# Decoder on one Trainium2 core: the masked-expert stage in two halves of the rows

## The reference

```python
# graph (_L0_xattn_ref): result is added to x, then layer norm
threshold = top_k(sim, 76)[0][:, :, -1:]
A_learned = sigmoid(sim) * (sim >= threshold)
A_learned = (A_learned + swapaxes(A_learned, -1, -2)) * 0.5
return (1.0 - gamma) * adj_raw + gamma * A_learned          # adj_raw is x
# experts (_L0_ffn_ref)
logits = einsum('bsd,ed->bse', x, router_w)
top1_w, top1_idx = max(softmax(logits)), argmax(softmax(logits))
w_q = clip(round(weight / 0.5), -1, 1) * scale[:, None]
out[token] = top1_w * (x[token] @ (w_q * expert_masks[top1_idx]).T)
```

## Time and profile before

| | |
|---|---|
| time, median of 3 runs | 870.21 us (869.89 to 872.01) |
| the profiled execution | 870.9 us |
| its span, first to last instruction | 869.1 us |
| TensorE busy | 790.7 us, 91% |
| VectorE busy | 572.8 us, 66% |
| ScalarE busy | 422.1 us, 49% |
| GpSimd busy | 498.7 us, 57% |
| mean granted TensorE clock | 0.968 |
| chain that ended last | PE 66%, DVE 14%, issue 7%, POOL 5% |

### The profile page before, as it was taken

The page is one execution under the profiler, slowest core; times in us unless marked ns, Lnnn a source line. Parts: engine busy times, 40 slices in busy tenths (PEclk is TensorE's granted clock), DMA queues, the critical chain, the costliest instruction groups (busy, mean ns, idle before and its releaser), DMA issues.

```text
span 869.1 us, 14599 instructions
## 1 busy us (share of the span) xinstructions
PE 790.7 (91%) x4731; PEld 678.7 (78%) x4737; DVE 572.8 (66%) x1661; ACT 422.1 (49%) x1193; POOL 498.7 (57%) x407
## 2 busy tenths in 40 slices
PE   8999999999999876794899989999985899999995
PEld 5878898888888864492788878898874588888884
DVE  5796876967768486123778878786737645455555
ACT  3473644636446564171475745766754532323232
POOL 6667468647587351512585546356512387776763
PEclk9999999999999997797999999999999899999998
DMA  7121620222316112555020111010001011111111
GB/s 215 66 98 35 208 97 1 97 68 80 123 35 194 62 56 68 193 113 140 0 79 3 54 55 56 1 55 26 25 1 38 13 55 36 54 36 54 46 32 49
DMA packets 58332, 59.09 MB, mean 68 GB/s; under 512 B 5392, under 2 KB 49312, under 8 KB 58272
## 3 DMA queue, kind: packets, MB, share of 16 engines
q1 hardware_dynamic: 57504, 56.24, 20.8%
q0 software_dynamic: 768, 2.10, 0.8%
HBM read 50.00 MB, written 8.32 MB: 67 GB/s over the span
## 4 chain that ended last, share of the span: by engine, by line
PE 66%; DVE 14%; issue 7%; POOL 5%; DVEq 2%; ACT 2%; DMA 2%; POOLq 1%; SPq 0%
PE bank L126 15%; PE bank L128 15%; PE bank L127 15%; PE bank L913 4%; PE bank L946 4%; PE bank L907 3%; PE bank L927 3%; DVE bank L1174 2%; PE bank L947 2%; POOL a_queries L755 2%; DVEq L1221 2%; DVE a_top L1223 1%; PE bank L1652 1%; PE bank L1653 1%; DVE sim L1149 1%
## 5 line engine op out<-in xcount | busy, mean ns | idle before, releaser
L1054 ACT ACTIVATE a_probs<-bank,a_neg_peak 128x128 f32<-128x128 f32 (+1 forms) x256 | 103.5, 429 | 96.2 <-DVE a_neg_peak L1174 96.2
L1174 DVE CUSTOM_DVE_ANT_0 bank<-bank,causal 128x128 f32<-128x128 f32 (+1 forms) x256 | 82.6, 390 | 34.2 <-PE bank L907 32.8
L1082 ACT ACTIVATE a_probs<-a_probs,a_row_inv 128x128 f32<-128x128 f32 (+1 forms) x256 | 92.1, 454 | 11.2 <-DVE a_row_inv L1182 11.2
L1060 ACT ACTIVATE a_probs_t<-bank 128x512 f32<-128x512 f32 x96 | 54.1, 601 | 60.3 <-PE bank L927 60.3
L946 PE MATMUL bank<-a_probs_t,a_vals 128*128 128x256 f32 x256 | 77.7, 386 | 3.3 <-DVE a_ot_lo L1194 3.3
L1909 POOL TENSOR_TENSOR d_h_lo<-d_h,d_h_hi 128x512 fp32r<-128x512 f32 x40 | 51.7, 1294 | 45.5 <-ACT d_h_hi L2029 31.9
L755 POOL TENSOR_TENSOR a_queries<-sim 128x512 f32<-128x512 f32 x32 | 41.0, 1283 | 62.3 <-DVE sim L1149 62.3
L126 PE MATMUL bank<-a_wo_hi,a_ot_hi 128*128 128x256 f32 x256 | 72.8, 284 | 4.3 <-issue 4.3
L2115 DVE TENSOR_TENSOR d_h<-d_silu,bank 128x512 f32<-128x512 f32 x40 | 27.5, 688 | 71.9 <-PE bank L128 70.5
L128 PE MATMUL bank<-a_wo_hi,a_ot_lo 128*128 128x256 f32 x256 | 71.7, 280 | 0.0
L127 PE MATMUL bank<-a_wo_lo,a_ot_hi 128*128 128x256 f32 x256 | 71.6, 280 | 0.0
(11 more groups left out here) (328 smaller groups left out, 2410.1 us busy)
## 6 DMA issues: line engine op xcount, KB each, us to landing
d_raw<-in_L_ffn_we_dram SPq DMA_DIRECT2D x48, 128.0 KB, 2.2
raw_k<-in_L_attn_w_k_dram SPq DMA_DIRECT2D x8, 512.0 KB, 7.4
raw_q<-in_L_attn_w_q_dram SPq DMA_DIRECT2D x8, 512.0 KB, 6.4
raw_v<-in_L_attn_w_v_dram SPq DMA_DIRECT2D x8, 512.0 KB, 7.6
raw_o<-in_L_attn_w_o_dram SPq DMA_DIRECT2D x8, 512.0 KB, 3.6
kv<-_L_ffn_expert_masks_dram SPq DMA_DIRECT2D x16, 256.0 KB, 3.0
kvt<-_L_ffn_expert_masks_dram SPq DMA_DIRECT2D x16, 256.0 KB, 3.1
raw_o<-in_L_attn_Wo_dram SPq DMA_DIRECT2D x8, 512.0 KB, 3.6
```

The lines of the kernel that those rows point to most:

```text
L1054: nc.scalar.activation(probs[s % 2][:, i, at:at + width], c.banks[i][:, at:at + width], ACT.Exp, bias=neg_peak[:, n:n + 1], scale=-1.0, ac ...
L1082: last = nc.scalar.activation(part, part, ACT.Copy, scale=row_inv[:, s % 2, n + r:n + r + 1])
L1174: last = nc.vector.tensor_tensor_reduce(part, part, mask, -1.0, 3e38, ALU.add, ALU.min, neg_peak[:, n + r:n + r + 1])
```

## The change

The rows are grouped in halves. Each half has its own sorted list (`sorted_rows[h]`, `y_sorted[h]`), of 39 tiles and five chunks, so there are ten chunks and 78 tiles. A class `Grouping` holds the steps of the chain for one half.

Half 0's chain moves into the first attention, to the ends of steps: constants and the first tanh (6), keep (7), turns, symmetric and the moments (8), first_norm (9), second_norm (10), turn of x (11), raw router products and flatten (12), logits and choose (13), rank, put, weigh and find (14); GpSimd scatters it in step 15, ahead of its last masks. The units use the ring. In the masked stage half 1's chain runs beside the weight turns and the first chunks; its scatter lies beside half 0's chunks; half 0's gather, sums and norm lie beside half 1's chunks. The keep_warm calls of the stage are gone, the products' banks are three instead of four, bank 3 serves the router.

```diff
+KEPT_STEP, FLAT_STEP, X_STEP, LOGITS_STEP, RANK_STEP = 8, 12, 11, 13, 14
+EARLY = {KEPT_STEP: ("kept", 0, range(B // 2)), X_STEP: ("turn", 0, range(KC)), FLAT_STEP: ("raw", 0, range(1)),
+         LOGITS_STEP: ("logits", 0, range(1)), RANK_STEP: ("rank", 0, range(1))}
...
@@ attention, SyncE @@
-                if not rope and g == 2:
-                    blank = c.idle[:].bitcast(F32).unsqueeze(1).broadcast_to([P, CHUNKS * BANK // P, D])
-                    sp.dma_start(c.sorted_rows.rearrange("(t p) d -> p t d", p=P), blank).then_inc(c.s_blank, 16)
+                if not rope and g == 1:
+                    sp.dma_start(grouping.numbers[:], a["numbers"][:, 0:HALF_NT]).then_inc(grouping.s_numbers, 16)
+                if not rope and g in (2, 3):
+                    blank = c.idle[:].bitcast(F32).unsqueeze(1).broadcast_to([P, HALF_CHUNKS * BANK // P, D])
+                    sp.dma_start(c.sorted_rows[g - 2].rearrange("(t p) d -> p t d", p=P), blank).then_inc(c.s_blank[g - 2], 16)
...
@@ attention, GpSimd, in step s, ahead of masks(s) @@
                 if not rope and s == 9:
                     ternary()
+                    pool.drain()
+                    grouping.norm1.root(pool, 0, factor=c.less_sq[:])
+                if not rope and s == 10:
+                    grouping.norm2.root(pool, 0)
+                if not rope and s == LAST:
+                    grouping.scatter(pool, 0)
...
@@ attention, TensorE, at the end of step s @@
+                if s == KEPT_STEP:
+                    kept_transposes(0)
+                elif s == X_STEP:
+                    for k in range(KC):
+                        grouping.turn(pe, 0, k, claim("turn", 0, k), s_early_t)
+                elif s == FLAT_STEP:
+                    pe.wait_ge(s_taken, taken("turn", 0, KC - 1))
+                    grouping.raw(pe, 0, claim("raw", 0, 0))
+                elif s == LOGITS_STEP:
+                    grouping.logits(pe, 0, claim("logits", 0, 0))
+                elif s == RANK_STEP:
+                    grouping.rank(pe, 0, claim("rank", 0, 0))
...
@@ attention, ScalarE, at the end of step s @@
+                if s == KEPT_STEP - 2:
+                    tanh(0)
+                elif s == X_STEP:
+                    for k in range(KC):
+                        act.wait_ge(s_early_t, k + 1)
+                        nc.scalar.activation(c.xt_hi[:, k, 0:HALF], ring_bank("turn", 0, k)[:], ACT.Copy).then_inc(s_early_hi, 1)
+                elif s == FLAT_STEP:
+                    grouping.flatten(act, 0, ring_bank("raw", 0, 0))
+                elif s == LOGITS_STEP:
+                    tanh(1)
+                elif s == RANK_STEP:
+                    grouping.exp(act, 0)
...
@@ attention, VectorE, at the end of step s @@
+                if s == KEPT_STEP - 2:
+                    grouping.constants(dve)
+                elif s == KEPT_STEP - 1:
+                    keep(0)
+                elif s == KEPT_STEP:
+                    symmetric(0)
+                    grouping.norm1.moments(dve, lambda t: c.x[:, t], 0)
+                elif s == KEPT_STEP + 1:
+                    grouping.first_norm(dve, 0)
+                elif s == KEPT_STEP + 2:
+                    grouping.second_norm(dve, 0)
+                elif s == X_STEP:
+                    for k in range(KC):
+                        dve.wait_ge(s_early_hi, k + 1)
+                        nc.vector.tensor_tensor(c.xt_lo[:, k, 0:HALF], ring_bank("turn", 0, k)[:], f32(c.xt_hi[:, k, 0:HALF]), ALU.subtract).then_inc(s_taken, 1)
+                elif s == FLAT_STEP:
+                    dve.wait_ge(grouping.s_flat, 1)
+                    nc.vector.memset(grouping.total[:], 0.0).then_inc(s_taken, 1)
+                elif s == LOGITS_STEP:
+                    grouping.choose(dve, 0, ring_bank("logits", 0, 0), s_taken)
+                elif s == RANK_STEP:
+                    grouping.put(dve, 0, ring_bank("rank", 0, 0), s_taken)
+                    grouping.weigh(dve, 0)
+                    grouping.find(dve, 0)
...
                 if not rope and s == LAST - 1:
-                    keep(range(NT))
+                    keep(1)
...
-TILES0 = 47
+TILES0 = 39
+HALF_CHUNKS = -(-TILES0 // CHUNK)
+CHUNKS = 2 * HALF_CHUNKS
...
+    def first_norm(self, dve, h):
+        c = self.c
+        self.norm1.wait(dve, h)
+        for t in HALF_TILES[h]:
+            self.nc.vector.scalar_tensor_tensor(c.x[:, t], c.x[:, t], self.norm1.rstd[:, t:t + 1], c.sim[:, t], ALU.mult, ALU.add)
+        dve.drain()
+        self.norm2.moments(dve, lambda t: c.x[:, t], h)
...
@@ masked stage, SyncE @@
+            def load(q):
+                if q in TAKEN_FROM:
+                    sp.wait_ge(s_xt, XT + KC * (TAKEN_FROM[q] + 1))
+                sp.dma_start(sorted_x[q], c.sorted_rows[q // HALF_CHUNKS][q % HALF_CHUNKS * BANK:(q % HALF_CHUNKS + 1) * BANK].rearrange("(t p) d -> p t d", p=P)).then_inc(s_sorted[load_of[q % HALF_CHUNKS]], 16)
...
+            sp.wait_ge(s_masked, PAIRS)
+            sp.wait_ge(grouping.s_scattered[0], 16 * HALF_NT)
+            for q in range(0, 2):
+                load(q)
+            sp.wait_ge(s_turned, 8)
+            for q in range(2, HALF_CHUNKS):
+                load(q)
             sp.wait_ge(s_turned, PAIRS)
             weights.first_loads(sp, "kqv")
+            for r in range(0, 6):
+                store(r)
+            sp.wait_ge(grouping.s_scattered[1], 16 * HALF_NT)
+            for q in range(5, 7):
+                load(q)
...
@@ masked stage, GpSimd @@
-            norm1.roots(pool, c.less_sq[:])
-            norm2.roots(pool)
+            grouping.norm1.root(pool, 1, factor=c.less_sq[:])
+            grouping.norm2.root(pool, 1)
+            grouping.scatter(pool, 1)
             pool.wait_ge(s_turned, PAIRS)
             weights.first_splits(pool)
+            weights.gather(pool, 0)
             weights.second_splits(pool)
...
@@ masked stage, TensorE @@
             for pair in range(0, 11):
                 turn(pair)
+            for k in range(KC):
+                grouping.turn(pe, 1, k, c.banks[6 + k], s_xt)
+            for pair in range(11, 14):
+                turn(pair)
+            pe.wait_ge(s_xt_lo, XT)
+            grouping.raw(pe, 1, SIDE)
             for pair in range(14, PAIRS):
                 turn(pair)
+            grouping.logits(pe, 1, SIDE)
-            keep_warm(c, 24)
-            pe.wait_ge(s_scattered, 16 * NT)
-            keep_warm(c, 10)
+            pe.wait_ge(grouping.s_column, 1)
             pe.wait_ge(s_w, PAIRS)
             turn_chunk(0)
             for q in range(CHUNKS):
                 if q + 1 < CHUNKS:
                     turn_chunk(q + 1)
+                if q == HALF_CHUNKS:
+                    pe.wait_ge(grouping.s_column, 2)
                 products(q)
-            keep_warm(c, 15)
-            turned3.pe(pe, s_norm3, 4, range(1))
-            keep_warm(c, 6)
+                if q == 0:
+                    grouping.rank(pe, 1, SIDE)
+                if q == CHUNKS - 2:
+                    turned3.pe(pe, s_norm3, HALF_NT, range(1))
...
@@ masked stage, VectorE @@
+            grouping.norm1.moments(dve, lambda t: c.x[:, t], 1)
+            grouping.first_norm(dve, 1)
+            grouping.second_norm(dve, 1)
...
+            grouping.choose(dve, 1, SIDE, s_done)
+            low(0)
+            low(1)
+            grouping.put(dve, 1, SIDE, s_done)
+            low(2)
+            grouping.weigh(dve, 1)
+            grouping.find(dve, 1)
+            for q in range(3, CHUNKS - 1):
+                low(q)
             weights.sums(dve, HALF_TILES[0])
+            low(CHUNKS - 1)
```

459 lines of the change are left out of this document (267 added, 192 removed).

## The result

The changed kernel takes **884.82 us** (median of 4 runs, 881.63 to 885.76), the kernel before 870.52 us (869.89 to 872.01) beside it: ratio 1.0155, 95% interval 1.0126 to 1.0184. It is 14.3 us slower; forecast were 1.7 us slower and a range up to 880. The profiled execution of the changed kernel took 881.63 us, the shortest of the four.

A forecast was written before the change was run, and what follows sets the result against it. The second pass was taken as bound by TensorE with VectorE hardly trailing; +18.9 us there and -17.2 in the masked stage made +1.7 on 870.2, about 872 us, range 861 to 880.

The forecast's parts named there:

- hand-over: First attention's second pass: 0.3 us of slack before the second value tile, so VectorE work delays TensorE nearly one for one.
- Rival (a): Second pass: ring's lead and VectorE's idle 6.6 us per pair absorb the added work; 862 us, chance 0.30.
- Shared SBUF port: 0 to 2.4 us, I take +1.2: Second pass, step 7: keep falls beside GpSimd's output split and waits for one running split to end; +1.2 us.
- by that rule alone all twenty such operations could wait, +5 more: Second pass: all twenty added VectorE operations with two SBUF inputs could wait for GpSimd; estimated +5 us, not in the sum.
- Last two steps, +2.7: End of second pass: put, weigh and find delay pv(15) by 3.9 us; halved turns and symmetric leave the end +2.7.
- Steps 9 to 11, 4.5: Second pass: half 0's first_norm and second_norm add 5.2 us on VectorE, less 0.7 of waits: +4.5 us.
- 11 to 13, 3.4: Second pass: turn of x, copy and subtraction 1.9 us, raw bank's wait for flatten 2.2, less 0.7: +3.4 us.
- Queues of GpSimd and SyncE at nothing: Second pass: the queued root delays K and Q splits and weight loads within some 12 us of slack; cost 0.
- Masked stage to chunk 5: From S, the attention's last addition to x: half 1's x S+15.4, first product S+26.7, chunk 5 S+47.3 after 1.8 stall.
- Norm 3 at S+71.7: Masked stage: half 0's gather, sums and third norm lie beside chunks 5 to 8; VectorE delivers about S+71.7, stage ends S+76.6.
- Clock in the stage, +1.5: Masked stage: without keep-warm products TensorE may run at 1.2 GHz after idling and ahead of chunk 0; +1.5 us.
- Rival (b): Masked stage: TensorE enters chunk 0 at the low clock and stays so through chunks 0 and 1; +6, 878 us, chance 0.15.

The follow-up runs named there:

- e11: Changed kernel with GpSimd's output splits held, constants next to keep(0), top-k search without copies, added work left at ends of steps: 873.31 us.
- e2b: Changed kernel with constants, keep, first_norm and second_norm of half 0 between value copies and output additions, GpSimd's value splits and last output split held: 873.62 us.
- e0: The changed kernel run a second time, nothing altered: 884.68 us.
- e1: Changed kernel with GpSimd's output splits of groups 4 and 7 held until keep(0) and half 0's choose are done: 878.17 us.
- e10: Changed kernel with 22 keep-warm products ahead of the turn of half 1's x and 20 ahead of the last turn: 880.63 us.

## Why the prediction was wrong

By its own steps:

- **Bound: right; hand-over: right in kind, wrong in place.** VectorE's added work came through nearly one for one (e11: 18.0 for 17.7). TensorE waits 1.87 us ahead of the query projection at 194.7 and 2.27 us ahead of its own added turns at 203.1, where the kernel before had no gap; in front of the value tiles, where the forecast had the gap, it is 0.25 to 0.93 us, once 0.71 in the kernel before. The attention's end at 339.3 lies above the 330 to 337 that were given. Rival (a), absorption, fell; what fills idle time has to be put there, and e2b shows that it then fits.
- **"Shared SBUF port: 0 to 2.4 us, I take +1.2": the term that failed.** keep lost 3.1 us (5.54 for 2.4), choose 1.7, the copy of step 12 2.2, while that of step 10 lost 1.1 less than before: 5.9 us in the profiled execution, 4.7 above the price. I had reasoned from the earlier trace rows that one running split has to end first. But a series of operations waits anew for each GpSimd operation; chosen and the copies, which I had as plain, have a port too; and e0 shows another 4.0 us on the constants. The sentence "by that rule alone all twenty such operations could wait, +5 more" was set aside as a remote bound, and it was the better number. The kernel before held a row that could have told it (225.51, 1.77 us for a copy that takes 0.28 elsewhere); it stands 3.5 us behind the windows of the earlier trace rows.
- **Last two steps, +2.7: came as 4.9.** The pv subtraction of step 15 lost 3.5 us against step 14's, near the 3.9 written down (its own terms, 7.3 less 2.4 less the wait of 1.51, give 3.4). But I gave back 1.2 us for halved turns and additions, and instead the last outputs ran at 1.2 GHz behind a wait of 3.72 us. I had priced the clock only in the masked stage. Port and tail are 4.7 and 2.2 us above their prices, 6.9 together; 4.5 are missing, so the other terms were 2.4 too high.
- **Steps 9 to 11, 4.5, and 11 to 13, 3.4: came as 3.0 and 4.9.** The shares are off mostly by the two copies named; the wait of the raw bank (2.0 measured, 2.2 worked out) was right.
- **Queues of GpSimd and SyncE at nothing: right.** No split of K, Q, V or O releases TensorE in steps 8 to 13; e1 and e2b delay splits by some 3 to 4 us and get faster.
- **Masked stage to chunk 5: right** within 0.4 us at each mark.
- **Norm 3 at S+71.7: came at S+75.0.** I let VectorE deliver it "beside chunks 5 to 8", without its order: the sums stand behind chunk 8's low part, and their first operation meets a split (1.27 for 0.41). (The sum behind it is also off by 0.4: 71.7, a turn of 1.1 and 3.4 make 76.2, not 76.6.)
- **Clock in the stage, +1.5: 3.2 by e10.** Rival (b) had the right mechanism and the wrong place.
- **Range:** of its upper cases none summed the small ones, and 884.8 lies above all of them. Port and clock both act on everything that is late, so their cost grows with the number of meetings; the range should have reached the +5 of the rule.

## What to carry to other kernels

Before work is put on VectorE, list what GpSimd runs at that moment, and price every two-input, copy or scalar operation within SBUF with the rest of the GpSimd operation beside it, one wait for each in a series. Idle time on an engine is only free if the other engine of the port is held away from it; where its result isn't needed soon, a semaphore wait or two do it (6.5 us in e1, 11 in e2b). Look then at what the delayed operation meets: in e1 it was the next copy. If the runs of a kernel spread more than those of its predecessor, look for two engines, neither of which waits for the other, that share something, and compare two profiles of the same kernel. And after each wait of TensorE look at the clock of the stretch behind it.
